# Fusion stage of a many-layer model on one core: gate products moved among the turnings, copies ahead of exponentials, value products moved up, fills left out

## What is computed

```python
qf = elu(xn @ W_q_lin + b_q_lin) + 1.0
kf = elu(xn @ W_k_lin + b_k_lin) + 1.0
vl = xn @ W_v_lin + b_v_lin
kv = einsum('bsd,bse->bde', kf, vl)
lin_out = einsum('bsd,bde->bse', qf, kv)
lin_out = lin_out / (einsum('bsd,bd->bs', qf, kf.sum(axis=1))[..., None] + 1e-06)
...
gate_in = concatenate([lin_out, win_out, xn], axis=-1)
gate = sigmoid(relu(gate_in @ W_g1 + b_g1) @ W_g2 + b_g2)
fused = gate * lin_out + (1.0 - gate) * win_out
return fused @ W_out + b_out + residual
```

## Time and profile before

| | |
|---|---|
| median of 3 runs | 1926.74 us (1926.43 to 1928.82) |
| profiled execution, its own time | 1924.38 us |
| its span, first to last instruction | 1922.7 us |
| PE busy over the span | 1710.8 us (89%) |
| DVE / ACT / POOL busy | 1113.9 / 803.8 / 513.9 us |
| the stage of the change | from 971.9 to about 1211 us of the span |
| fills (L130) of 128 x 512 in the whole kernel | 496 records, 141.5 us |

### The profile page before, as it was taken

The page is one execution under the profiler, slowest core; times in us unless marked ns, Lnnn a source line. Parts: engine busy times, 40 slices in busy tenths (PEclk is TensorE's granted clock), DMA queues, the critical chain, the costliest instruction groups (busy, mean ns, idle before and its releaser), DMA issues. The chain is left out here.

```text
span 1922.7 us, 37555 instructions
## 1 busy us (share of the span) xinstructions
PE 1710.8 (89%) x13524; PEld 1254.7 (65%) x13616; DVE 1113.9 (58%) x3105; ACT 803.8 (42%) x1538; POOL 513.9 (27%) x483
## 2 busy tenths in 40 slices
PE   7899969997787699989889887899998999889997
PEld 5678759986666599867756554222224887558886
DVE  2477842226999522268844557688886677862221
ACT  1255413323553111135533345799994454211111
POOL 1000112215302143152000112555552001233553
PEclk9999969998998699989989889899999999989998
DMA  6000245531003455312010013899992002115662
GB/s 226 1 1 0 117 131 187 178 112 28 20 0 124 129 188 176 113 34 71 30 44 1 18 40 123 321 388 377 357 331 107 1 0 86 60 44 160 188 195 45
DMA packets 97421, 228.43 MB, mean 119 GB/s; under 512 B 24297, under 2 KB 55753, under 8 KB 96393
## 3 DMA queue, kind: packets, MB, share of 16 engines
q1 hardware_dynamic: 77527, 206.92, 30.6%
q0 software_dynamic: 19552, 19.63, 4.3%
q10 hardware_dynamic: 210, 0.15, 0.0%
HBM read 199.69 MB, written 26.56 MB: 118 GB/s over the span
## 5 line engine op out<-in xcount | busy, mean ns | idle before, releaser
L2387 ACT ACTIVATE l2s_hidden<-ps,pack_l2f 128x816 f32<-128x816 f32 x256 | 226.8, 937 | 18.6 <-PE ps L2311 9.1
L130 PE MATMUL ps<-pack_const 128*128 128x512 bf16 x496 | 141.5, 418 | 31.5 <-PEq L164 6.1
L2406 POOL TENSOR_TENSOR l2s_gated<-l2s_hidden,l2s_whole 128x408 f32<-128x408 f32 x128 | 136.7, 1069 | 103.5 <-PE ps L2319 103.5
L2429 DVE TENSOR_TENSOR l2s_gated<-l2s_hidden,l2s_whole 128x816 f32<-128x816 f32 x128 | 142.8, 1116 | 27.4 <-ACT l2s_hidden L2387 25.7
L1927 PE MATMUL ps<-l_down,l_hidden 128*128 x792 | 139.8, 326 | 0.0
L1886 POOL DMA_INDIRECT l_xt<-rows_in,l_tokens x66 | 63.1, 956 | 252.6 <-PE ps L1899 194.1
L1927 PEld LDWEIGHTS ps<-l_down,l_hidden 128*128 128x128 f32 x792 | 127.3, 190 | 0.4
L130 PEld LDWEIGHTS ps<-pack_const 128*128 128x128 bf16 x588 | 57.3, 105 | 88.5 <-issue 48.3
L1910 PE MATMUL ps<-l_xtT,l_up 128*128 128x128 f32 x792 | 100.3, 277 | 3.4 <-DVE l_xtT L2162 3.4
L1910 PEld LDWEIGHTS ps<-l_xtT,l_up 128*128 128x128 f32 x792 | 97.5, 193 | 4.4 <-DVE l_xtT L2162 4.4
L2006 ACT ACTIVATE l_hidden<-ps,l_down 128x128 f32<-128x128 f32 x198 | 54.6, 374 | 90.1 <-PE ps L1915 90.1
(11 more groups left out here) (479 smaller groups left out, 3936.6 us busy)
## 6 DMA issues: line engine op xcount, KB each, us to landing
l2s_whole<-g_whole SPq DMA_DIRECT2D x128, 612.0 KB, 6.8
l_up<-in_l_up SPq DMA_DIRECT2D x66, 576.0 KB, 3.8
l3c_wg<-in_l_gate SPq DMA_DIRECT2D x16, 576.0 KB, 5.0
l3c_wu<-in_l_up SPq DMA_DIRECT2D x16, 576.0 KB, 6.6
l3c_wd<-in_l_down SPq DMA_DIRECT2D x16, 576.0 KB, 3.9
slots_out<-l_y SPq DMA_DIRECT2D x66, 96.0 KB, 2.3
l_down<-in_l_down SPq DMA_DIRECT2D x8, 675.0 KB, 8.7
l_down<-in_l_down SPq DMA_DIRECT2D x8, 576.0 KB, 7.3
```

The lines of the kernel that those rows point to most:

```text
L130: pe.matmul(bank, halves[:, 0:128], halves[:, :], start=True, stop=True)
L2387: act.activation(hidden[:, p % kept, :, :], ps[:, 0, 2 * (p % 2):2 * (p % 2) + 2, 0:NG], ACT.Gelu_apprx_tanh, bias=w.at("b1")[:, s * MT + ...
L2406: pool.tensor_tensor(gated[:, (4 * n + 1) % ring, :], hidden[:, 2 * n % kept, 1, :], whole[:, n % ahead, 0, :], ALU.mult).then_inc(late_re ...
L2429: dve.tensor_tensor(gated[:, at:at + 2, :], hidden[:, (2 * n + 1) % kept, :, :], whole[:, n % ahead, 1:3, :], ALU.mult).then_inc(gated_rea ...
```

## The change

PSUM banks: half co = 0 of the first gate product is now summed in bank (1,0) instead of (0,0), so that it no longer shares a bank with the turnings; co = 1 stays in (0,1). With that:

- The two parts of half 0 that come from `xT_all` (n = 4, 5) are issued between the turnings of tiles 1 and 2, where four fills stood; the two fills ahead of tile 3 are gone as well. `gate_hidden` then adds parts 0 to 3 of half 0, each behind a wait for its own copy instead of for all four, and makes half 1 as before. `lin_scores`, which writes bank (1,0), gets a wait for ACT's ReLU of half 0.
- ACT runs `mix_copies` ahead of `lin_exponentials` instead of behind it.
- PE runs `lin_values(q)` ahead of `step(at[0])` instead of behind it, and the 10 fills of that step are left out for t = 0 and 4 (they stay for t = 8 and 12).
- `fused_transposes` keeps its 10 fills (and the wait for `gate_in` ahead of them) for group 0 alone.

In all 24 + 30 + 20 = 74 fills go. No product and no copy is added or removed.

```diff
+        def hid_bank(co):
+            return ps[0:K, 0, 1, 0:NG] if co else ps[0:K, 1, 0, 0:NG]
+
...
             def lin_scores(q):
                 pe.wait_ge(lin_f_ready, q + 1)
+                if q:
+                    pe.wait_ge(hid_ready, 2 * (q - 1) + 1)
...
+            def hidden_part(q, co, n, start=False, stop=False):
+                part = mixT[:, n, :] if n < 2 * C else turned(q, n - 2 * C)
+                return pe.matmul(hid_bank(co), w.at("wg1", 3 * C)[:, n, co * K:(co + 1) * K], part, start=start, stop=stop)
+
             def mix_transposes(q):
                 pe.wait_ge(lin_o_ready, q + 1)
                 if q:
                     pe.wait_ge(y_added, q)
                 for n in range(2 * C):
+                    if n == 2:
+                        if q + 1 < G:
+                            pe.wait_ge(lin_x_ready, 4 * (q + 2))
+                        hidden_part(q, 0, 2 * C, start=True)
+                        hidden_part(q, 0, 2 * C + 1)
                     if n >= 2:
-                        if n == 2 and q + 1 < G:
-                            pe.wait_ge(lin_x_ready, 4 * (q + 2))
-                        fill(pe, g, ps[:, 1, 0, :], 4 if n == 2 else 2)
                         pe.wait_ge(mixT_ready, 4 * q + n - 1)
...
             def gate_hidden(q):
 
-                pe.wait_ge(mixT_ready, 4 * (q + 1))
-                parts = [mixT[:, n, :] for n in range(2 * C)] + [turned(q, c) for c in range(C)]
-                for co in range(C):
-                    for n, part in enumerate(parts):
-                        last = pe.matmul(ps[0:K, 0, co, 0:NG], w.at("wg1", 3 * C)[:, n, co * K:(co + 1) * K], part,
-                                         start=(n == 0), stop=(n == 3 * C - 1))
-                    last.then_inc(hid_ps, 1)
+                for n in range(2 * C):
+                    pe.wait_ge(mixT_ready, 4 * q + n + 1)
+                    last = hidden_part(q, 0, n, stop=(n == 2 * C - 1))
+                last.then_inc(hid_ps, 1)
+                for n in range(3 * C):
+                    last = hidden_part(q, 1, n, start=(n == 0), stop=(n == 3 * C - 1))
+                last.then_inc(hid_ps, 1)
...
             def fused_transposes(q):
 
-                pe.wait_ge(gate_in, q + 1)
-                fill(pe, g, ps[:, 0, 0, :], 10)
+                if q == 0:
+                    pe.wait_ge(gate_in, q + 1)
+                    fill(pe, g, ps[:, 0, 0, :], 10)
                 pe.wait_ge(fused_ready, q + 1)
...
-                    if t % GB == 0:
-                        if t // GB + 2 < G:
-                            pe.wait_ge(lin_x_ready, 4 * (t // GB + 2) + 2)
+                    if t % GB == 0 and t // GB + 2 >= G:
                         fill(pe, g, ps[:, 1, 1, :], 10)
                     pe.wait_ge(z_ready, t + 1)
...
                 if q < G:
                     lin_products(q)
+                    lin_values(q)
                 step(at[0])
-                if q < G:
-                    lin_values(q)
...
                 step(at[0])
+                if 1 <= q <= G:
+                    mix_copies(q - 1)
                 if q < G:
                     lin_exponentials(q)
                 if 1 <= q <= G:
-                    mix_copies(q - 1)
                     hidden(q - 1)
```

2 lines of the change are left out of this document (1 added, 1 removed).

## The result

The changed kernel takes **1908.73 us** (median of 4 runs, 1908.16 to 1909.16) against 1927.78 for the kernel before, measured beside it (median of 4, 1926.43 to 1936.5): a ratio of 0.9897, 95% interval 0.9874 to 0.9921. The profiled execution took 1908.65, its span is 1906.9.

A forecast was written before the change was run, and what follows sets the result against it. No single engine bounds the stage: PE in a round's first half, the ACT - DVE - POOL chain in the second. 2.05 + 4.6 + 3.3 + 1.8 - 1.7 = 10.05 us off, giving 1916.7; range 1911.5 to 1922.0.

The forecast's parts named there:

- Units: Unit costs at the full clock: 0.69 us for one part (two records) of gate_hidden, about 0.22 a fill, 0.087 a turning.
- round 1: Turnings and gate_hidden of round 1: six fills and the 0.60 wait ahead of gate_hidden go; gain 2.05 us.
- round 2: Ten fills ahead of step(0) go (2.16 us), turnings and gate_hidden lose 2.5 of fills and waits; gain 4.6 us.
- rival 4: Reordering gives less: lin_scores waits for late features, 2 us in each of three rounds come back; about 1922, chance 0.07.
- Round 3: Turnings and gate_hidden of round 3: tile 2 starts 0.9 us earlier, fewer fills and waits, low clock begins anew; gain 3.3.
- Round 4: Turnings and gate_hidden of round 4: low clock holds at first, six fills and a wait go; gain 1.8 us.
- The loss in round 4: Missing fills ahead of out_products of round 4 leave PE some 3 us idle, so those products run low; loss 1.7 us.
- The limit of 1 us: Sign of being wrong altogether: stages outside the changed one change by more than 1 us.
- step(3), (7) and (11): Sign in these steps: each waits longer for ACT's copy of z, its L1338 products starting no earlier relative to DVE's fuse.
- Rival 1: Low clock ends sooner in rounds 3 and 4, no gap left in turnings and gate_hidden; 12 to 15 less, chance 0.15.
- Rival 2: More low clock: out_products of rounds 3 and 4 and one block fall low; 5 to 7 left, about 1920.5, chance 0.20.
- rival 3: Clock falls at the turnings in front of gate_hidden, two of four blocks wholly low in addition; about 1931, chance 0.05.

The follow-up runs named there:

- the four positions: Changed kernel and kernel before, each with 0, 4, 8 or 12 more fills ahead of lin_products of round 2; stage difference 13.9 us on average.
- the gap fills: Changed kernel with more fills where PE waits anyway: first fused_transposes, step(8), step(12), and step(3), (7), (11); 1903.51 us, ratio 0.9883.

## Why the prediction was wrong

The direction was right, and so were the fills, the waits and the order of work, which are about 12.3 of the stage's 16.75. What failed is the clock. The size was forecast at 10.05 and is 18 to 19, and the two steps that failed are the low stretches of rounds 3 and 4, which I took over from the kernel before.

- **Units, round 1, round 2: right.** 2.05 against 2.14 and 4.6 against 4.72. In both, 9.7 us of work was to stay and 9.63 did, with no wait for ACT's copies. `lin_scores` waits for nothing in rounds 1 to 3, so rival 4 is out.
- **Round 3: the waits were right, the clock was not.** Tile 2 waits 3.08 for ACT ("some 3 us"), the copies stand right behind step(4), and tile 2 is turned 1.27 earlier in relation to the round's start (0.9 forecast). The step that failed is "because the low clock begins anew after the idle time": I kept the low stretch of the earlier trace rows whole behind a longer wait. It was half as long, 3.4 us for 6.8. From tile 2's turning to step(5) the changed kernel takes 9.34 against 13.24; the term is 5.17 instead of 3.3, and 3.6 to 5.2 over the four positions (4.6 as a mean).
- **Round 4: the step that failed most.** "The low clock holds at first" was read off turnings that were busy for 1.57 in the earlier trace rows. In the changed kernel the low stretch ends before the block begins. The block gives 4.72 for 1.8, and step(8) in front of it, which I gave no term, 1.70. These two and round 3 are 6.5 of the 8.0 us by which the time was missed; what else I did not count leaves about 1.4 (0.7, 1.5 and 1.4 gained, 1.7 and 0.5 lost). In before step(8) stood wholly low, and I had not looked at where that stretch began: a low stretch ahead of an edited place was taken as given, although everything ahead of it had moved by 11 us. Much of this miss is luck of position: over the four positions the block gives 2.5 and step(8) loses 0.5, so 1.8 was wrong for the kernel as it is and not far off as a mean.
- **The loss in round 4: right in place and size.** Gap 2.82 ("some 3"), `out_products` 5.11 busy (5.3), loss 2.25 (1.7). But with the fused fills put back the clock falls in step(12) and the stage is as long in the traced execution, so there the loss isn't a net price of leaving them out.
- **Not counted: `out_products` of round 1**, low at 4.53, a loss of 1.68. I had checked low clock for the rounds with missing fills; in round 1's `fused_transposes` the fills stay. It comes with the parts in a bank of their own, since they alone show it, and at every position. With 16 fills for 10 ahead of it (the gap fills) it is 2.86 again.
- **The rest of the stage** gave 1.5, and the stretch behind it 1.4, which I had said would prove me wrong altogether. The limit of 1 us was too narrow for such a sign: with the same code, the stretch behind the stage takes about 709.8 us in eight of the 18 traces and 711.1 to 711.9 in the other ten. The changed kernel with the fused fills back is at 711.2 and one of before is at 709.9, so it doesn't go with the change. It is the clock once more, some 430 to 480 us behind the stage, but it is 1.4 us that I left out of the sum.
- **step(3), (7) and (11)** were to wait longer for ACT's copy of z. True of rounds 3 and 4 (1.90 and 2.82); in round 2 the wait is 1.76 where it was 2.80. The low clock begins earlier there now, and step(3)'s products ahead of the wait take longer, which would fill part of it; no run tests that.
- **The rule from the Trainium skill**, "TensorE: Matmul & The Clock Gate", Part 4, that turnings don't count as activity, would have had round 3 fall low. It did not: its gap is 1.90, with turnings ahead of it, and `out_products` took 2.77. No run separates turnings from idle time, so whether the rule holds stays open; its price did not come due there.
- **Rivals.** Rival 1, the low clock ends sooner, with 12 to 15 less, named what happened in rounds 3 and 4, and had 0.15. Its reason (no gap left inside the block) fits round 3's order of rows; in round 4 the clock was up before the block began, so gaps in it can't be the reason. Its size was short as well, since it stopped at the blocks. Rival 2 took in the low `out_products` but in rounds 3 and 4; it came in rounds 1 and 4. (By its own terms it leaves a gain of 4.4 to 6, not 5 to 7.) PEclk in the blocks of rounds 1 and 2 is 1.00, so rival 3 did not happen in the changed kernel. Something like it did in round 2 of two others, with the value products moved up alone and with the exponential first, each time at the end of a wait for ACT's copies (2.81 and 2.31 us). The second of these differs from the changed kernel in ACT's order alone, so here it is that order which keeps round 2's block at the full clock.

What I can't settle is why the clock falls where it does in either kernel. The runs show that the places mostly repeat and that an offset of 1 to 3 us of the work behind them moves them; what sets them was not found, and so the 2.9 us of position could not have been forecast from the rows of before. What these runs teach is the width of the range: two edits that only took fills out or moved products changed the low-clock time of the stage by 17 and 14 us, 7 to 8 us of time. A range of 8 on either side of the sum, for the clock alone, would just have held the result; mine had 5.2. That is known only after the fact.

## What to carry to other kernels

Independent products in a bank of their own between a PE step and the copies it waits for are worth more than fills in the same place: they cover the wait and shorten what follows (13.4 us of the stage for the parts alone, 6.4 for leaving all the fills out). Put fills only where PE waits for another engine anyway (4.8 us less of the stage here, 2.8 of it left at the kernel's end); on PE's path each costs its 0.22 us, and leaving all of them out costs part of the gain in clock. Edits that belong together should be tried apart as well: the value products moved up lost 3.2 us of the stage alone, where ACT's order had not been changed with them. Where a low stretch stands ahead of or inside an edited place, price the place at either clock and widen the range by the difference, and measure the edit at two or three shifted positions before reading a few microseconds as its own.

## What the runs showed of the hardware that I had not expected

- The places of the low clock mostly repeat: two executions of the changed kernel have it at the same distances from the stage's start, with stages of 222.68 and 222.79. One trace of 18 had it elsewhere ahead of any edit, and took 1.4 us more for round 0.
- They are sensitive: 1.7 us of fills where nothing waits make the changed kernel's stage 3.5 longer and leave that of before as it was (239.43 and 239.19); 2.6 us make the changed one's 6.2 longer.
- A low stretch that is prevented in one place may come later in another: at step(12) with the fused fills back, at the same stage time, and behind step(9) in the kernel before shifted by 8, which gains 5.8 in step(8) and the block and loses 4.6 behind them.
- ACT's table load of 1.28 us stands in front of that exponential; behind the copies no PE wait in round 2 shows it, ahead of them it is part of PE's wait of 2.31.
